# Cross-attention and quantized FFN on one core: x of the last three pairs transposed in 32x32 blocks on VectorE, by way of DRAM

## The reference

```python
x = x + attention(layernorm(x), ctx, Wq, bq, Wk, bk)
#   Q = ln(x) Wq + bq,  K = ctx Wk + bk,  softmax(Q K^T / 32) ctx
x = x + ffn(layernorm(x), qweight, qzeros, scales, bias, g_idx)
#   weights = scales[g] * (sign(4-bit weight) - zeros[g]),  out = x @ weights + bias
```

## Time and profile before

| | |
|---|---|
| median of 3 runs | 586.87 us (586.83 to 587.43) |
| the profiled execution: its own time / its span | 587.93 us / 586.1 us |
| share of the span that PE, DVE, ACT, POOL are busy | 98%, 64%, 37%, 32% |
| stages in the trace: projection, T stage, the rest | 104.85, 200.07, 281.23 us |
| TensorE clock granted | 1.00 of 2.4 GHz throughout |

### The profile page before, as it was taken

How to read it: one execution, slowest core, us unless ns; L and a number is a source line. 1 busy time by engine, 2 the same in 40 slices (tenths; PEclk the granted TensorE clock), 3 DMA queues, 4 the chain that set the end, 5 groups by cost and what they waited for, 6 DMA issues and landing times.

```text
span 586.1 us, 7738 instructions
## 1 busy us (share of the span) xinstructions
PE 575.9 (98%) x2894; PEld 478.1 (82%) x2894; DVE 376.0 (64%) x621; ACT 215.1 (37%) x408; POOL 187.4 (32%) x135
## 2 busy tenths in 40 slices
PE   7999999999999999999999999999999999999997
PEld 6778888777877877788888999988778888888886
DVE  4688774488669649855013555595996767668442
ACT  6684444311512332233237666555232132122210
POOL 2053000000000000000125976676846724743630
PEclk9999999999999999999999999999999999999999
DMA  7852100031272342315415799897203311310111
GB/s 223 229 208 74 36 1 0 1 143 37 103 256 92 125 181 104 130 49 204 160 46 207 240 355 348 330 419 286 105 21 124 144 75 69 144 73 1 72 73 72
DMA packets 30868, 81.44 MB, mean 139 GB/s; under 512 B 2616, under 2 KB 10816, under 8 KB 28656
## 3 DMA queue, kind: packets, MB, share of 16 engines
q1 hardware_dynamic: 30832, 80.96, 38.1%
HBM read 53.69 MB, written 27.26 MB: 138 GB/s over the span
## 4 chain that ended last, share of the span: by engine, by line
PE 83%; DVE 8%; DMA 3%; ACT 3%; issue 2%; SPq 1%; POOL 0%; DVEq 0%; ACTq 0%
PE bank L1088 21%; PE bank L1090 21%; PE bank L1089 21%; PE bank L1133 4%; PE bank L1139 4%; PE bank L1136 4%; DMA wk_stage<-in_L_xattn_Wk 3%; PE bank L1099 2%; PE bank L1259 2%; PE bank L1189 2%; DVE stats L787 2%; DMA xin<-in_x 1%; DVE xres L959 1%; ACT wk_hi L508 1%; DVE yin L996 1%
## 5 line engine op out<-in xcount | busy, mean ns | idle before, releaser
L1088 PE MATMUL bank<-xT_hi,m_hi 128*128 128x512 f32 x256 | 105.3, 411 | 0.0
L1090 PE MATMUL bank<-xT_hi,m_lo 128*128 128x512 f32 x256 | 101.0, 395 | 0.0
L1089 PE MATMUL bank<-xT_lo,m_hi 128*128 128x512 f32 x256 | 100.8, 394 | 0.0
L452 POOL TENSOR_TENSOR pairs<-mv,pairs 128x2 f32<-128x2 f32 x16 | 11.1, 696 | 180.8 <-DVE mv L792 180.3
L1042 DVE TENSOR_TENSOR xres<-xres,bank 128x512 f32<-128x512 f32 x56 | 38.4, 686 | 46.2 <-PE bank L1090 46.1
L652 ACT ACTIVATE t_pair<-bank,ucol 128x512 f32<-128x512 f32 x32 | 22.0, 688 | 117.7 <-PE bank L1090 117.7
L483 POOL TENSOR_TENSOR l_lo_s<-l_sum_s,l_hi_s 128x512 fp32r<-128x512 f32 x32 | 42.4, 1359 | 71.2 <-DVE l_sum_s L978 71.2
L469 POOL TENSOR_TENSOR tT_lo<-t_pair,tT_hi 128x1024 fp32r<-128x1024 f32 x16 | 39.2, 2466 | 68.1 <-ACT tT_hi L508 68.1
L1088 PEld LDWEIGHTS bank<-xT_hi,m_hi 128*128 128x128 f32 x256 | 48.2, 188 | 12.0 <-issue 0.2
L1090 PEld LDWEIGHTS bank<-xT_hi,m_lo 128*128 128x128 f32 x256 | 48.1, 188 | 11.3
L1089 PEld LDWEIGHTS bank<-xT_lo,m_hi 128*128 128x128 f32 x256 | 48.2, 188 | 10.7 <-issue 0.2
(11 more groups left out here) (137 smaller groups left out, 1277.0 us busy)
## 6 DMA issues: line engine op xcount, KB each, us to landing
xin<-in_x SPq DMA_DIRECT2D x8, 1024.0 KB, 6.1
cin<-in_ctx SPq DMA_DIRECT2D x8, 1024.0 KB, 5.6
xres<-in_x SPq DMA_DIRECT2D x8, 1024.0 KB, 10.8
out<-xres SPq DMA_DIRECT2D x15, 512.0 KB, 2.6
right_scratch<-part_hi SPq DMA_DIRECT2D x28, 256.0 KB, 2.2
r_tile<-right_scratch SPq DMA_DIRECT2D x6, 1024.0 KB, 10.9
r_tile<-right_scratch SPq DMA_DIRECT2D x3, 1536.0 KB, 8.6
right_scratch<-part_lo_t SPq DMA_DIRECT2D x16, 256.0 KB, 2.1
```

The lines of the kernel that those rows point to most:

```text
L1088: pe.matmul(out_, a_hi, b_hi, start=start, stop=False, skip_group_check=True)
L1089: pe.matmul(out_, a_hi, b_lo, start=False, stop=False, skip_group_check=True)
L1090: return pe.matmul(out_, a_lo, b_hi, start=False, stop=stop, skip_group_check=True)
```

## The change

Pair 0 is still transposed on PE. For batches 2 to 7 there are no PE transposes. Instead:

- raw rows of batch 2 are loaded into a buffer of their own (`xraw`), those of batches 3 to 7 into the first half of `xin`; `x_apply` writes the normalized rows into the second half, with the features reordered in groups of 32, and `row_terms` reads them with a copy of `wrow` in that order (`wrow_q`, two more ACT copies);
- SP stores these rows to DRAM (`store_xn`) and loads them back with four DMAs (`load_quadrants`), each to 32 partitions, in pieces of 256 numbers;
- DVE transposes each batch in place by one instruction of 128x2048 elements (`x_blocks`), and `x_hi` and `x_lo` read the SBUF tile `xq` instead of PSUM;
- the numbers of the hand-written orders change: the first four gathers and the first two `right_sums` are one step later, and dictionaries place `x_stats`, `x_apply` with `row_terms`, `x_blocks`, the stores and the reloads.

```diff
-        GATHER = {2: 0, 4: 1, 8: 2, 10: 3, 15: 4, 17: 5, 21: 6, 23: 7}
-        SUMS = (6, 12, 19, 25)
+        GATHER = {3: 0, 5: 1, 9: 2, 11: 3, 15: 4, 17: 5, 21: 6, 23: 7}
+        SUMS = (7, 13, 19, 25)
...
-            X_TR[p, NB - 2, NB - 1] = (0, 1)
-            X_TR[p, NB - 1, 4] = (2, 3)
-            X_TR[p, NB - 1, NB - 1] = (4, 5)
-            X_TR[p + 1, 0, 3] = (6, 7)
+        X_STATS = {1: 3, 8: 4, 10: 5, 16: 6, 18: 7}
+        X_APPLY = {0: 2, 2: 3, 9: 4, 11: 5, 17: 6, 19: 7}
+        X_BLOCKS = {3: 2, 5: 3, 12: 4, 14: 5, 21: 6, 22: 7}
+        STORE_XN = {n: (b,) for n, b in X_APPLY.items()}
+        QUADRANTS_BACK = {1: (2,), 3: (3,), 10: (4,), 12: (5,), 19: (6,), 20: (7,)}
...
+            def load_raw(b):
+                if b == 2:
+                    sp.wait_ge(s_m, 2 * NB)
+                elif b == 3:
+                    sp.wait_ge(s_xtr, NB)
+                    sp.wait_ge(s_dot, 1)
+                else:
+                    sp.wait_ge(s_xn, QT * b)
+                sp.dma_start(xraw if b == 2 else xin[:, 0, :, :], x_rows[b]).then_inc(s_xraw, 16)
+            def store_xn(b):
+                sp.wait_ge(s_xn, QT * (b + 1))
+                sp.dma_start(xn_dram[b].rearrange("(t p) f -> p t f", p=P), xin[:, 1, :, :]).then_inc(s_xst, 16)
+            def load_quadrants(b):
+                sp.wait_ge(s_xst, 16 * (b - 1))
+                if b == B - 2:
+                    sp.wait_ge(s_xn, QT * B)
+                if b == B - 1:
+                    sp.wait_ge(s_dot, B)
+                rows = xn_dram[b].rearrange("(m j) f -> j m f", j=32)
+                for a in range(4):
+                    sp.dma_start(xq[b // 2][32 * a:32 * a + 32, b % 2 * NB:(b % 2 + 1) * NB, :],
+                                 rows[:, :, a * S:(a + 1) * S]).then_inc(s_xql[b % 2], 16)
...
                     for k, i in LO_AT.get(n, ()):
                         store_right(k, i, True)
+                    for b in STORE_XN.get(n, ()):
+                        store_xn(b)
+                        if 3 < b + 1 < B:
+                            load_raw(b + 1)
+                    for b in QUADRANTS_BACK.get(n, ()):
+                        load_quadrants(b)
...
-                copy(wrow[:, h * HALF:(h + 1) * HALF], bank[4 + h][:, :]).then_inc(s_wrow, 1)
+                copy(wrow[:, h * HALF:(h + 1) * HALF], bank[4 + h][:, :])
+                copy(by_quadrant(wrow_q)[:, KH * h:KH * (h + 1), :, :],
+                     bank[4 + h][:, :].rearrange("q (k a i) -> q k a i", k=KH, a=4)).then_inc(s_wrow, 1)
...
+            def x_blocks(b):
+                dve.wait_ge(s_xql[b % 2], 64 * (b // 2))
+                tile = xq[b // 2][:, b % 2 * NB:(b % 2 + 1) * NB, :].rearrange("p m f -> p (m f)")
+                dve.transpose(tile, tile).then_inc(s_xT, 1)
...
+            x_stats(2)
             row_terms(0)
             row_terms(1)
...
-                    if p < PAIRS - 1:
-                        if j in (2, 3):
-                            x_stats(2 * p + j)
-                            x_apply(2 * p + j)
-                        if j in (4, 5):
-                            row_terms(2 * p - 2 + j)
+                    if n in X_STATS:
+                        x_stats(X_STATS[n])
+                    if n in X_APPLY:
+                        x_apply(X_APPLY[n])
+                        row_terms(X_APPLY[n])
+                    if n in X_BLOCKS:
+                        x_blocks(X_BLOCKS[n])
...
-                        for u in X_TR.get((p, j, i), ()):
-                            x_tr(p + (j > 0), u)
```

More of the change, by code:

```diff
@@ L133, in xattn_ffn_kernel @@
         xin = at("xin", 162.25, [P, 2, QT, D], F32)
-        wrow = at("wrow", 178.25, [P, D], F32)
-        uacc = wrow
+        xq = [None] + [at(f"xq{p}", kb, [P, 2 * NB, S], F32) for p, kb in ((1, slot[2]), (2, slot[4]), (3, 162.25))]
+        xraw = at("xraw", slot[5], [P, QT, D], F32)
+        wrow = at("wrow", 82, [P, D], F32)
+        uacc = at("uacc", 178.25, [P, D], F32)
+        wrow_q = uacc
         packed = at("packed", 182.25, [P, D], I32)
@@ L196, in xattn_ffn_kernel @@
         s_stat, s_rstd, s_xn, s_dot = sem("ln_stats"), sem("ln_rstd"), sem("xn_done"), sem("row_terms")
+        s_xraw, s_xst = sem("x_of_later_pairs_loaded"), sem("xn_stored")
+        s_xql = [sem(f"xn_reloaded{i}") for i in range(2)]
+        s_xT = sem("xn_transposed_by_blocks")
         s_xtr, s_xhi, s_xlo = sem("xn_transposed"), sem("xT_hi_done"), sem("xT_lo_done")
@@ L233, in wq_split_count, with by_quadrant @@
             return 2 * h + b + 1 if b < 2 else 2 * b + h + 1
+        def by_quadrant(rows):
+            return rows.rearrange("q (a k i) -> q k a i", a=4, k=NB)
         def c_bank(b, u):
@@ L363, in _ @@
                     n = NB * p + j
[L364 to L368, removed]
                     if n == NB * (PAIRS - 1) + 1:
@@ L554, in x_hi @@
             def x_hi(p, u):
[L555 removed]
                 if p == 0:
+                    act.wait_ge(s_xtr, u + 1)
                     act.wait_ge(s_wqused, NB)
[L558 to L562 removed]
+                    copy(xT_hi[:, u, :], bank[6 + u % 2][:, :]).then_inc(s_xhi, 1)
+                else:
+                    act.wait_ge(s_xT, 2 * p)
+                    if u < NB - 1:
+                        act.wait_ge(s_xused, (NB - 1) * (p - 1) + u + 1)
+                    else:
+                        act.wait_ge(s_t, NB * p)
+                    copy(xT_hi[:, u, :].rearrange("p (m j) -> p m j", j=32), xq[p][:, :, 32 * u:32 * u + 32]
+                         ).then_inc(s_xhi, 1)
             for b in range(NB):
@@ L804, in x_apply, with x_stats @@
-            def x_apply(b):
-                ln_apply(xin[:, b % 2, :, :], b, s_xn)
+            def x_stats(b):
+                if b < 2:
+                    dve.wait_ge(s_xl[b], 16)
+                    ln_stats(xin[:, b, :, :])
+                else:
+                    dve.wait_ge(s_xraw, 16 * (b - 1))
+                    ln_stats(xraw if b == 2 else xin[:, 0, :, :])
+            def x_apply(b):
+                dve.wait_ge(s_rstd, b + 1)
+                if b == 2:
+                    dve.wait_ge(s_xtr, NB)
+                elif b > 2:
+                    dve.wait_ge(s_xst, 16 * (b - 2))
+                for t in range(QT):
+                    if b < 2:
+                        out_, in_ = xin[:, b, t, :], xin[:, b, t, :]
+                    else:
+                        out_, in_ = by_quadrant(xin[:, 1, t, :]), (xraw if b == 2 else xin[:, 0, :, :])[:, t, :].rearrange(
+                            "q (k a i) -> q k a i", k=NB, a=4)
+                    dve.tensor_scalar(out_, in_, mv[:, t, 0:1], rstd[:, t:t + 1], ALU.subtract, ALU.mult).then_inc(s_xn, 1)
@@ L852, in row_terms @@
                         i = QT * b + t
-                        order.link(dve.tensor_tensor_reduce(junk, xin[:, b % 2, t, cols], wrow[:, cols], 1.0, 0.0,
-                                                            ALU.mult, ALU.add, cdot[:, h, i:i + 1]))
+                        order.link(dve.tensor_tensor_reduce(junk, xin[:, min(b, 1), t, cols], (wrow if b < 2 else wrow_q)[:, cols],
+                                                            1.0, 0.0, ALU.mult, ALU.add, cdot[:, h, i:i + 1]))
                 cols = slice(QT * b, QT * (b + 1))
@@ L1090, in three, with x_tr @@
                 return pe.matmul(out_, a_lo, b_hi, start=False, stop=stop, skip_group_check=True)
[L1092 to L1095, removed]
+            def x_tr(u):
+                pe.wait_ge(s_xn, 4)
+                wait(pe, s_xlo, u - 1)
                 for bt in range(2):
```

27 lines of the change are left out of this document (11 added, 16 removed).

## The result

The changed kernel takes 592.48 us (median of 5 runs, 590.56 to 593.75), the kernel before 586.87; the ratio is 1.009, with a 95% interval of 1.0069 to 1.0111. That is 5.6 us slower and clear of the noise, where 586.1 and no measurable change were forecast. The forecast's range, 582.9 to 592.5, just ends there.

A forecast was written before the change was run, and what follows sets the result against it. PE was taken as the bound, busy 575.9 of 586.1 us. Removing 10.5 us of transposes and 0.8 of old waits against 10.5 of new waits gave -0.8: 586.1 from the median 586.87, range 582.9 to 592.5.

The forecast's parts named there:

- What is removed: On PE, 96 of 128 transposes go, 10.5 us, and 0.8 us of old gather waits for weights.
- The pieces on DVE: Durations in DVE's queue: row_terms 3.5 us, x_apply 1.45, block transpose 2.2, half a weights 1.3, right_sums 2.7.
- The reload: Four 256 KB DMAs bringing a batch back from DRAM: 6.6 us, the middle between 4.7 and 8.4.
- Where PE will wait: DVE's new order laid against PE's steps in the T stage: 10.5 us of new waits in all.
- Step 4: PE has gathered and waits 3.1 us for weights, behind x_apply, row_terms and the block transpose on DVE.
- Step 22: PE waits 3.4 us for weights, behind splits held up by store, reload and small stores.
- Steps 10 to 12: PE waits 1.9 us together for weights, behind row_terms(4), the late load of batch 5, and x_apply(5) with row_terms(5).
- Ends of pair 0 and step 3: PE waits 0.4 us for late splits at steps 7 to 8, and 0.6 for block 0's one-hot tile.
- Step 23: PE waits 1.1 us for weights, as the next store hangs behind the reload of batch 7.
- with 5.57 a step, 0.45 a gather and the waits as they come: How PE's times were counted on from the start of step 1, 111.81, in us.
- The reload becomes the bound: Rival: a reload takes 8.4 us, waits grow by about 8 us, time 594; slower side, chance 0.33.
- All of it gained: Rival: DVE has 73 us free, only 13 added, so PE gains 10.5 + 0.8: 575.6; chance 0.03.

The follow-up runs named there:

- the last experiment: Changed kernel with all its tables of places set anew and row_terms placed apart from x_apply, the work the same; 575.79 us, ratio 0.9823.
- the first pause: Kernel before, with TensorE made to wait for unread DVE block transposes behind steps 24, 26 and 28, here the one behind 24; 604.01 us, ratio 1.0287.
- the fillers: Changed kernel with matmuls nobody reads ahead of the two longest-waiting gathers, 14 at step 4 and 17 at step 22; 589.94 us, ratio 1.0053.

## Why the forecast was wrong

- **What is removed** was right: 11.2 us by the last experiment, 11.3 by the sum.
- **The pieces on DVE** were right: block transpose 2.24 start to start (2.2), `row_terms` 3.51 (3.5), `x_apply` of the reordered kind 1.57 start to start (1.45), in itself as long as the plain one. **The reload** was near for an empty queue, 6.9 in the last experiment where 6.6 was taken, but short for the changed kernel: 7.6 for batch 2, with the next store issued before it had landed, and 7.7 for batch 3, behind a load.
- **Where PE will wait** was right in place and 1.6 us short in size: 12.1 us by the gaps between matmuls, 10.5 forecast. Step 4: 3.85 (3.1), of which 0.65 is the hole for POOL's operation; the sum had taken `x_stats` at 3.0, "if other work fills the 0.8", and the `pick` that was to fill it ran while POOL's operation took 1.30 us in place of 0.69. Step 22: 4.88 (3.4), of which 1.0 is from the queue of store, reload and small stores, 10.8 us (237.10 to 247.87) where 9.8 was counted. Steps 10 to 12: 2.4 (1.9). Ends of pair 0 and step 3: 0.7 and 0.3 (0.4 and 0.6). Step 23: none (1.1): `weights` ended at 259.96, and PE's step ended at 262.3, 2.5 of it by the slow matmuls, so that at full clock it would have waited some 0.2, by an estimate from these rows.
- **The step that failed** is the one by which PE's times went on "with 5.57 a step, 0.45 a gather and the waits as they come". A step behind a wait of 4 to 5 us did not take 5.57: its matmuls ran at 1.2 GHz for nearly 6 us. The price of the clock behind a long wait was put at nothing. It was 5.2 us in two places, of the 7.0 by which the T stage missed its forecast (206.24 to 199.3); 1.6 more are the longer waits. No row of the kernel before could show it, since its longest wait is 1.3 us and its granted clock 1.00; but the Trainium skill, page "TensorE: Matmul & The Clock Gate", section "HAM oscillation — how this bites in real kernels", warns of long idle gaps between matmuls, and it was not weighed. The windows above agree with it for the two long waits: 0.61 as the wait ended, 0.50 behind it. The falls behind waits of 2 us and less, in the experiments, go beyond what it warns of. With the 5.2 in the sum the forecast would have been 591.3, and with the 1.6 of waits 592.9.
- **The rivals.** None named the clock. "The reload becomes the bound" gave about the right time, 594, mostly for another reason. The reload did pass the 7.5 that it names, but by the forecast's own prices 1.0 us more a reload gives 588.1. The waits that it put at step 6 and at the end of pair 1 did not come, reloads into 128 partitions took only 1.5 us of waits away, and putting the small stores behind the reloads did away with the wait at step 22 though the reloads were still into 32. That the measured time lies inside the range at all is luck: the range reached 592.5 for dear block transposes and slow reloads, and the transposes were not dear. "All of it gained", with 0.03, was out of reach for the order as it was; its bound, 575.6, is what the same work gives in another order, 575.79. The wait at step 4, held against it as fixed by the transpose's length, went when the pieces of DVE's queue were placed otherwise.

## What to carry to other kernels

A wait of TensorE, where it bounds the stage, can cost more than its length: here 8.7 us of waits in two places brought 5.2 more behind them, so a sum of new waits needs a term for the clock behind each long one. In these traces it was 1.4 to 2.9 us behind waits of 3.2 us and more, and it did not grow with the wait. Work moved to an engine that is idle a third of the time is not free until each piece has a place at which nobody waits behind it in the queue; try the places before giving up the change, since moving two numbers of a table was worth 12.1 us and the rest of them 4.6. Read counts beside busy shares: 11 matmuls in a full window where 17 fit is how a slow clock looks.

## What the runs showed of the hardware that was not expected

- The granted clock read 0.61 in the two microseconds in which a wait of 3.85 us ended, 0.50 behind it, and was full again after 5.9 us of work; matmuls of 128x512 followed each other at 0.43 us in place of 0.23. Behind the same wait in another run it was full again after 4.1 us of work, and 1.6 us were lost in place of 2.7. It fell with little DMA traffic too (share 0.47 in the one window, 0.00 in the other). It also fell behind three short ones, 1.9 us (the first pause), 1.9 (what the fillers left at step 22) and 2.0 (the projection of the last experiment's trace), though not behind others of 1.99, 1.84 and 1.66.
- The same reload, four DMAs of 256 KB in runs of 1 KB, landed behind a load after 7.7 us into 32 partitions each and after 6.5 into 128; into an empty queue after 6.9 and 5.8.
- A block transpose of 128x2048 float32 on DVE takes 2.30 us, 1.12 ns an element, near the pace of the elementwise rows (1.20 and 1.36 ns) and not that of the reduction (1.96). By the Trainium skill, page "Vector Engine (DVE) Microarchitecture Reference", section 3.8, it was 2.1 by an estimate; the runs say 0.2 more.
- POOL's operation on 128x2 numbers took 1.30 us while DVE ran `pick`, 1.07 while it ran two splits, and 0.69 where DVE stood idle or ran `weights`. Why is not tested here.
